# Context gate from two taps with three products per token pair, and the mixture gate's sums on VectorE

## What is computed

```python
ctx = causal_ema(x, tau_ctx)                       # h[t] = alpha * h[t-1] + x[t]
wg = sigmoid(concat([x, ctx], -1) @ Wg.T + bg)     # "wgate"
gated = x * wg
h1 = gelu(x @ Wn1.T + bn1)                         # "mod_hidden"
mod = 0.5 + sigmoid(h1 @ Wn2.T + bn2)              # "mod", one row per average
traces = [causal_ema(gated * mod[d], tau_raws[d]) for d in range(8)]
temporal = sum(traces[d] * softmax(blend, 0)[d] for d in range(8))
gate = sigmoid(temporal @ Wtemp.T + btemp)         # "tgate"
soma = gelu(x @ Wsoma.T + bsoma)
out = (soma * gate) @ Wout.T                       # "out"
x = x + layernorm(out) * gamma + beta

s0, s1, s2 = (relu(x @ share_wi[i]) @ share_wo[i] for i in range(3))
expert_out = two experts of the image's type, weighted by wa and wb
gi = concat([expert_out[:, 0], s0[:, 0], s1[:, 0], s2[:, 0]], -1)
g = softmax(relu(gi @ gate_w1) @ gate_w2, -1)      # the mixture's gate: one row of four per image
x = x + expert_out * g[0] + s0 * g[1] + s1 * g[2] + s2 * g[3]
```

## Time and profile before

| | |
|---|---|
| median of 3 runs | 1036.35 us (1035.94 to 1036.43) |
| the profiled execution | 1037.89 us, its span 1035.9 us |
| TensorE busy | 1029.4 us, 99% of the span, 4784 matmuls |
| VectorE busy | 806.9 us, 78% |
| ScalarE busy | 415.5 us, 40% |
| GpSimd busy | 16.4 us, 2% |
| moved to and from memory | 223 MB, 215 GB/s over the span |

### The profile page before, as it was taken

One profiled execution on the slowest core, in us unless ns is written; L12 is line 12 of the kernel. 1 busy time (PEld: TensorE's weight loads), 2 busy tenths in 40 slices (PEclk: granted clock), 3 DMA queues, 4 the chain that ended last, 5 costly groups with the idle time before them and its releaser, 6 DMA issues.

```text
span 1035.9 us, 12766 instructions
## 1 busy us (share of the span) xinstructions
PE 1029.4 (99%) x4784; PEld 853.9 (82%) x4784; DVE 806.9 (78%) x1369; ACT 415.5 (40%) x695; POOL 16.4 (2%) x26
## 2 busy tenths in 40 slices
PE   9999999999999999999999999999999999999998
PEld 6688888888888888888888888888888888888898
DVE  6989977799767988489785997659976699745236
ACT  7654455533344234422434233442333423333232
POOL 1200000000000000000000000000000000000000
PEclk9999999999999999999999999999999999999999
DMA  6388999786454754465544664546645475456581
GB/s 214 123 294 287 299 366 373 291 303 236 152 203 153 264 193 163 162 235 204 208 166 159 242 234 146 196 164 245 215 149 203 163 258 201 142 191 216 200 323 74
DMA packets 38304, 223.02 MB, mean 215 GB/s; under 512 B 4515, under 2 KB 5283, under 8 KB 16611
## 3 DMA queue, kind: packets, MB, share of 16 engines
q1 hardware_dynamic: 35938, 209.63, 56.9%
q0 software_dynamic: 2304, 12.58, 3.2%
HBM read 188.51 MB, written 33.69 MB: 215 GB/s over the span
## 4 chain that ended last, share of the span: by engine, by line
PE 95%; DMA 2%; DVE 2%; issue 0%; ACT 0%; SPq 0%; DVEq 0%
PE ps_up L680 14%; PE ps_up L710 14%; PE ps_up L711 14%; PE ps_down L752 14%; PE ps_down L753 14%; PE ps_down L756 14%; PE ps_aux L673 2%; PE ps_aux L674 2%; PE ps_aux L675 2%; DMA wi<-split_wi 1%; DVE y L1691 1%; DMA wo<-split_wo 1%; PE ps_aux L853 1%; PE ps_aux L850 1%; PE ps_aux L849 1%; PE ps_aux L833 1%
## 5 line engine op out<-in xcount | busy, mean ns | idle before, releaser
L1081 ACT ACTIVATE hid_hi<-ps_up 128x512 fp32r<-128x512 f32 (+1 forms) x336 | 193.6, 576 | 494.2 <-PE ps_up L680 493.4
L1344 DVE SCALAR_TENSOR_TENSOR hid_lo<-ps_up,hid_hi 128x512 fp32r<-128x512 f32 (+1 forms) x336 | 219.8, 659 | 170.6 <-ACT hid_hi L1081 169.9
L710 PE MATMUL ps_up<-x_hi_all,wi 128*128 128x512 f32 (+1 forms) x660 | 250.3, 381 | 0.3 <-DMA wi<-split_wi 0.3
L711 PE MATMUL ps_up<-x_hi_all,wi 128*128 128x512 f32 (+1 forms) x660 | 249.9, 380 | 0.0
L752 PE MATMUL ps_down<-hid_hi,wo 128*128 128x512 f32 (+1 forms) x640 | 245.4, 384 | 0.2
L753 PE MATMUL ps_down<-hid_hi,wo 128*128 128x512 f32 (+1 forms) x640 | 245.1, 384 | 0.0
L680 PE MATMUL ps_up<-x_lo_all,wi 128*128 128x512 f32 (+1 forms) x660 | 197.3, 380 | 0.2 <-DVE x_lo_all L1335 0.2
L756 PE MATMUL ps_down<-hid_lo,wo 128*128 128x512 f32 (+1 forms) x640 | 193.7, 384 | 0.0
L710 PEld LDWEIGHTS ps_up<-x_hi_all,wi 128*128 128x128 f32 x660 | 124.1, 188 | 24.6 <-DMA wi<-split_wi 1.0
L711 PEld LDWEIGHTS ps_up<-x_hi_all,wi 128*128 128x128 f32 x660 | 124.1, 188 | 23.1
L680 PEld LDWEIGHTS ps_up<-x_lo_all,wi 128*128 128x128 f32 x660 | 122.0, 188 | 24.2 <-DVE x_lo_all L1335 0.4
(11 more groups left out here) (259 smaller groups left out, 898.0 us busy)
## 6 DMA issues: line engine op xcount, KB each, us to landing
wi<-split_wi SPq DMA_DIRECT2D x70, 1024.0 KB, 4.9
wo<-split_wo SPq DMA_DIRECT2D x70, 1024.0 KB, 4.9
modb<-mod_scratch SPq DMA_DIRECT2D x28, 512.0 KB, 5.9
split_wi<-wi SPq DMA_DIRECT2D x10, 1024.0 KB, 7.4
split_wo<-wo SPq DMA_DIRECT2D x10, 1024.0 KB, 8.0
xt<-in_x SPq DMA_DIRECT2D x8, 512.0 KB, 5.7
split_wi<-ex POOLq DMA_DIRECT2D x4, 1024.0 KB, 9.6
split_wo<-ex POOLq DMA_DIRECT2D x4, 1024.0 KB, 4.9
```

What stands on the lines that cost most here:

```text
L710: pe.matmul(ps, w_hi, x2_hi[:, parity, c, tokens], start=c == 0, stop=False)
L711: pe.matmul(ps, w_lo, x2_hi[:, parity, c, tokens], start=False, stop=False)
L1081: act.activation(hid_hi[:, k % NU, tokens], ps_up[k % NU][:, tokens], ACT.Relu).then_inc(hid_hi_ready, 1)
L1344: dve.scalar_tensor_tensor(hid_lo[:, k % NU, tokens], ps_up[k % NU][:, tokens], 0.0, f32(hid_hi[:, k % NU, tokens]), ALU.max, ALU.subtract ...
```

## The change

**The context gate.** For n = 2 to 7 the tokens are taken in pairs. `xg_hi` and `xg_lo` hold all even tokens first and then all odd ones; results are put back in order where they are read out (`evens_odds`, `apart`). With `A` the weights for the token itself and `G` those for the token before it, an odd token `o` behind an even one `e` needs `A o + G e`, an even one behind the odd `p` needs `A e + G p`. Both contain `(A + G) e`, which is made once per pair (`gate_mid`, 12 matmuls of 256 columns, slot 3.5); the rest is `A (o - e)` and `G (p - e)` (24 matmuls of 256 columns, in `wgate`). The differences (`next_steps`) are made by VectorE and split into high and low part like all inputs. ScalarE copies the sum of `gate_mid` out of PSUM, and VectorE adds it to each half before the scan. The sum of the weights is made once: three additions on GpSimd (`add_gate_weights`), a rounding copy on ScalarE and a remainder on VectorE (`mid_weights`).

**The gate of the mixture.** `gate_part_hi`, `gate_part_lo` and the matmuls of `gate_hidden` go. VectorE adds over the partitions with transposes of 32x32 blocks and sums along the free axis (`gate_units`, then `gate_logits`, seventeen instructions), each behind the one before by a semaphore where it needs its result. The weights `gw2` are laid out for this on the host.

```diff
 PLAN_TENSOR = {
-    0.5: ["mod_hidden"], 1.5: ["soma"], 2.5: ["mod", "gate_hidden"], 4.5: ["wgate"],
+    0.5: ["mod_hidden"], 1.5: ["soma"], 2.5: ["mod"], 3.5: ["gate_mid"], 4.5: ["wgate"],
 PLAN_SCALAR = {
-    1: ["mod_hidden_low", "gate_part_hi"], 1.5: ["mod_hidden"], 2: ["soma"], 3: ["mod_low"], 3.5: ["mod"], 4: ["gate_exp"], 5.5: ["wgate"],
+    1: ["mod_hidden_low"], 1.5: ["mod_hidden"], 2: ["soma"], 3: ["mod_low", "gate_exp"], 3.5: ["mod"], 4: ["gate_mid"], 5.5: ["wgate"],
-    36: ["next_x_hi"],
+    36: ["next_x_hi"], 37.5: ["next_steps_hi"],
 PLAN_VECTOR = {
-    0.5: ["gate_part"], 1: ["mod_hidden_sum"], 2: ["mod_hidden_lo", "gate_part_lo"], 3: ["mod_sum"], 3.5: ["gate_logits"],
-    4.5: ["gate_soft", "mix1"], 5: ["wgate_scan"], 5.5: ["mix2", "mix3"], 6: ["gated"], 6.5: ["mix0"],
+    0.5: ["gate_part"], 1: ["mod_hidden_sum"], 1.5: ["gate_units"], 2: ["mod_hidden_lo", "gate_logits"], 3: ["mod_sum"],
+    3.5: ["gate_soft"], 4.5: ["mix1"], 5: ["wgate_scan"], 5.5: ["mix2", "mix3"], 6: ["gated"], 6.5: ["mix0"],
-    36.5: ["next_x_lo"],
+    36.5: ["next_x_lo"], 37: ["next_steps"], 38: ["next_steps_lo"],
 FIRST_PLANS (scalar)
-               31: ["ln_sqrt"], 34.5: ["turn"], 35.5: ["x2_hi"], 37: ["next_x_hi", "table_gelu"]},
+               31: ["ln_sqrt"], 34.5: ["turn"], 35.5: ["x2_hi"], 37: ["next_x_hi", "table_gelu"], 38: ["mid_weights"], 39: ["next_steps_hi"]},
 FIRST_PLANS (vector)
-               37.5: ["next_x_lo"]},
+               37.5: ["next_x_lo"], 38.5: ["mid_weights", "next_steps"], 39.5: ["next_steps_lo"]},
 LAST_PLANS
-    "tensor": {41.5: ["gate_hidden"]}, ... 40: ["gate_part"], 42: ["gate_logits"],
+    "tensor": {}, ... 40: ["gate_part"], 40.5: ["gate_units"], 41.5: ["gate_logits"],
...
 TensorE
+                elif step == "gate_mid":
+                    if n == 2:
+                        pe.wait_ge(mid_weights, 5)
+                    pe.wait_ge(aux_free[1], p.aux[1]["gate_mid"])
+                    for m in range(CT):
+                        for c in range(CT):
+                            at = slice(c * E + m * P, c * E + (m + 1) * P)
+                            mm = product(ps_aux[1][:, half(m)], mid_hi[:, at], mid_lo[:, at], xg_hi[:, c, half(0)],
+                                         xg_lo[:, c, half(0)], m == 0 and c == 0, m == CT - 1 and c == CT - 1)
+                    mm.then_inc(aux_ready[1], 1)
+                elif step == "wgate" and n > 1:
+                    pe.wait_ge(steps_ready, (n - 1) * 3)
+                    for m in range(CT):
+                        pe.wait_ge(aux_free[m], p.aux[m]["wgate"])
+                        for s, w in enumerate((W_GATE, W_SUM)):
+                            for c in range(CT):
+                                at = slice(w + c * E + m * P, w + c * E + (m + 1) * P)
+                                mm = product(ps_aux[m][:, half(s)], wc_hi[:, at], wc_lo[:, at], steps_hi[:, c, half(s)],
+                                             steps_lo[:, c, half(s)], s == 0 and c == 0, s == 1 and c == CT - 1)
+                        mm.then_inc(aux_ready[m], 1)
...
 ScalarE
+                elif step == "next_steps_hi":
+                    act.wait_ge(steps_ready, (n - 1) * 3 + 1)
+                    hi(steps_hi, token_steps).then_inc(steps_ready, 1)
+                elif step == "mid_weights":
+                    act.wait_ge(mid_weights, 3)
+                    hi(mid_hi, mid_raw).then_inc(mid_weights, 1)
+                elif step == "gate_mid":
+                    act.wait_ge(steps_ready, (n - 1) * 3)
+                    act.wait_ge(aux_ready[1], p.aux[1]["gate_mid"] + 1)
+                    act.activation(gate_mid, ps_aux[1][:, :], ACT.Copy).then_inc(aux_free[1], 1)
...
 VectorE
+                elif step == "next_steps":
+                    dve.wait_ge(x_loaded[(n + 1) % 2], ((n + 1) // 2 + 1) * 16)
+                    dve.wait_ge(ema_sum, n * (2 * D))
+                    for c in range(CT):
+                        even, odd = (evens_odds(x_of(n + 1)[:, c, :])[:, s, :] for s in range(2))
+                        to_even, to_odd = (token_steps[:, c, half(s)] for s in range(2))
+                        dve.tensor_scalar(to_even[:, 0:1], even[:, 0:1], -1.0, None, ALU.mult)
+                        dve.tensor_tensor(to_even[:, 1:HALF], odd[:, 0:HALF - 1], even[:, 1:HALF], ALU.subtract)
+                        last = dve.tensor_tensor(to_odd, odd, even, ALU.subtract)
+                    last.then_inc(steps_ready, 1)
+                elif step == "next_steps_lo":
+                    dve.wait_ge(steps_ready, (n - 1) * 3 + 2)
+                    lo(steps_lo, token_steps, steps_hi).then_inc(steps_ready, 1)
+                elif step == "mid_weights":
+                    dve.wait_ge(mid_weights, 4)
+                    lo(mid_lo, mid_raw, mid_hi).then_inc(mid_weights, 1)
+                elif step == "wgate_scan" and n > 1:
+                    dve.wait_ge(aux_free[1], p.aux[1]["gate_mid"] + 1)
+                    for c in range(CT):
+                        dve.wait_ge(aux_ready[c], p.aux[c]["wgate"] + 1)
+                        dve.tensor_tensor(evens_odds(gates[:, c, :]), apart(ps_aux[c][:, :]),
+                                          gate_mid[:, half(c)].rearrange("p (s k) -> p s k", s=1).broadcast_to([P, 2, HALF]), ALU.add)\
+                            .then_inc(aux_free[c], 1)
+                        dve.wait_ge(aux_free[c], p.aux[c]["wgate"] + 1)
+                        dve.tensor_tensor_scan(gates[:, c, :], alpha[:, D:D + 1].broadcast_to([P, T]), gates[:, c, :], 0.0,
+                                               ALU.mult, ALU.add).then_inc(gate_scanned, 1)
...
 GpSimd
+            def add_gate_weights():
+                pool.wait_ge(wi_ready, UNITS - 1)
+                pool.wait_ge(wc_ready[1], 1)
+                for t, place in ((wc_lo, mid_raw), (wc_hi, mid_raw_part)):
+                    pool.tensor_tensor(place, f32(t[:, W_GATE:W_SUM]), f32(t[:, W_SUM:W_SOMA]), ALU.add).then_inc(mid_weights, 1)
+                pool.wait_ge(mid_weights, 2)
+                pool.tensor_tensor(mid_raw, mid_raw_part, mid_raw, ALU.add).then_inc(mid_weights, 1)
...
             for j in range(0, TILES, 2):
                 keep_tile(j)
                 keep_tile(j + 1)
                 if j + 2 < TILES:
                     load_tile(j + 2)
                     load_tile(j + 3)
+                if j == 2:
+                    add_gate_weights()
```

More of the change, by code:

```diff
@@ L109 @@
 LAST_PLANS = {
[L110 to L111 removed]
+    "sync": {47: ["store0"], 55.5: ["store1"]}, "tensor": {}, "scalar": {43: ["gate_exp"]},
+    "vector": {40: ["gate_part"], 40.5: ["gate_units"], 41.5: ["gate_logits"], 43.5: ["gate_soft", "final_scale"],
                44.5: ["final_early0"], 45: ["final_early1"], 45.5: ["final_early2"], 46: ["final_early3"],
@@ L133 @@
 EDGE1 = 16
-AUX_BANKS = {"mod_hidden": (0,), "mod": (1,), "gate_hidden": (0,)}
-GATING = {"gate_hidden", "gate_part_hi", "gate_part_lo", "gate_logits", "gate_exp", "gate_part", "gate_soft",
+GATE_CHAIN = 17
+AUX_BANKS = {"mod_hidden": (0,), "mod": (1,), "gate_mid": (1,)}
+GATING = {"gate_units", "gate_logits", "gate_exp", "gate_part", "gate_soft",
           "mix0", "mix1", "mix2", "mix3", "store", "store0", "store1", "final_scale", "final_expert_a", "final_expert_b",
@@ L304, in build @@
         wgate_ready = sem("wgate_ready")
+        steps_ready = sem("steps_ready")
+        gate_scanned = sem("gate_scanned")
+        mid_weights = sem("mid_weights")
         gated_ready = sem("gated_ready")
@@ L421, in build, with evens_odds, apart @@
         turned = temporal[:, :, :].rearrange("p c (t a j) -> p a c t j", t=TT, a=4)
+        token_steps, steps_hi, steps_lo = trace[:, :, :], ct_hi[:, :, :], ct_lo[:, :, :]
+        gate_mid = trace[:, 0, :]
+        mid_raw, mid_raw_part = (raw_wi[:, 0, i * CT * E:(i + 1) * CT * E] for i in range(2))
+        mid_hi, mid_lo = mid_parts[:, 0, :], mid_parts[:, 1, :]
+        def evens_odds(tokens):
+            return tokens.rearrange("p (k s) -> p s k", s=2)
+        def apart(columns):
+            return columns.rearrange("p (s k) -> p s k", s=2)
         def x_of(n):
@@ L865, in beside @@
                         mm.then_inc(aux_ready[c], 1)
-                elif step == "gate_hidden":
-                    if later(p.aux[0]["gate_hidden"]):
-                        pe.wait_ge(aux_free[0], p.aux[0]["gate_hidden"])
-                    if final(f):
-                        pe.wait_ge(gate_part, f * 8 + 8)
-                        pe.matmul(ps_aux[0][:, 0:E], ones[:, :], gpart[:, :], start=True, stop=True).then_inc(aux_ready[0], 1)
-                    else:
-                        pe.wait_ge(gate_part_hi_ready, f + 1)
-                        pe.matmul(ps_aux[0][:, 0:E], ones_r[:, :], gpart_hi, start=True, stop=False)
-                        pe.wait_ge(gate_part_split, f + 1)
-                        pe.matmul(ps_aux[0][:, 0:E], ones_r[:, :], gpart_lo, start=False, stop=True)\
```

(33 more changed lines are left out.)

57 lines of the change are left out of this document (31 added, 26 removed).

## The result

The changed kernel takes 1040.46 us (median of 6 runs, 1039.8 to 1041.0), against 1035.89 us for the kernel before on the same chip: ratio 1.0037, 95% interval 1.0024 to 1.005. It is 4.6 us slower. The forecast was +4.4 us and 1040.8 us. A second series on another occasion gave 1040.13 against 1035.66 us (1.0048, 1.0035 to 1.0062). The profiled execution took 1040.37 us, with a span of 1038.4 us. That span is only 2.5 us longer than that of before (1035.9), because the profiled execution of before was itself 2.0 us over the median of its kernel. From there to the end the changed kernel is 4.2 us longer.

The account below looks back on a forecast made before the run. TensorE's matmul stream was taken to bound the kernel. Span: 1035.9 - 6.9 - 1.7 + 10.8 + 2.2 + 0 = 1040.3 us, +4.4; on the median 1036.35 that gives 1040.8 us, range 1036.5 to 1045.

Parts of the forecast that it names:

- The gate product: Context gate's matmuls on TensorE in images n = 2 to 7: 1.15 us less per image, 6.9 us in all.
- `gate_hidden`: Two matmuls of 256 columns removed from TensorE, 0.24 us, seven times: 1.7 us less.
- The last image: Float32 `gate_hidden` gives back 0.55 us, the longer gate chain may delay TensorE: between -0.55 and +0.5, taken as 0.
- The wait at the passage: From image 0 to image 1, TensorE's `down(1, 0)` waits for VectorE's expert sum behind GpSimd's late additions: +10.8 us, once.
- The clock: TensorE's clock falls after the idle stretch between image 0 and image 1, slowing matmuls: 0 to 4.4 us, taken as +2.2.
- The moving averages: VectorE's two extra additions per middle image lag 0.27 us, covered by 0.74 us of slack before a late `hid_lo`: 0.
- The additions are not late: Rival, 12%: GpSimd's three sums are done before ScalarE asks, leaving 2.7 us of chain at the passage: 1030.5 us.
- The clock stays high: Rival, 14%: TensorE's clock does not fall after the idle stretch, so the 2.2 us drop out: 1038.6 us.
- Every second element costs more: Rival, 13%: strided operands slow VectorE, up to 3 us in middle images and 1 in the chain: 1042 to 1045 us.

Follow-up runs that it names:

- mixture_gate_alone: The kernel before with only the mixture gate's part of the change, its context gate as before: 1034.12 us, ratio 0.998.
- adds_early: The changed kernel with GpSimd's three weight additions moved ahead of its stores of tiles 2 and 3: 1031.17 us; repeated, 1031.41 us.
- store_later: adds_and_steps_early with SyncE's store of image 0's output moved from slot 8 to slot 16 of the second image: 1026.53 us, ratio 0.9912.
- engine_kept_busy: The changed kernel with 46 unused float32 matmuls on TensorE during its wait for the expert sum before down(1,0): 1037.61 us, ratio 1.0014.
- adds_and_steps_early: adds_early with the first image's token differences moved to slots 32.5 to 34.5 and the weights' rounding to 36.5: 1028.79 us; repeated, 1028.23 us.
- one_addition_more: The changed kernel with a fourth, unused addition of 128x512 on GpSimd between the second and third: 1041.28 us, ratio 1.005.

## Why the prediction was right, and where it was off

- *The gate product, -6.9 us.* Right: 1.13 us an image against a forecast of 1.15, six images, 6.8 us.
- *`gate_hidden`, -1.7 us.* Right: 0.25 us an image, and 1.9 us for this part alone. The seventeen instructions took 3.7 us beside image 4 of the changed kernel, for an estimate of 3.4, and made nobody wait in the middle images.
- *The last image, 0.* The middle of the stated range, and about right. In the traces of the changed kernel and of mixture_gate_alone TensorE has one wait there that it didn't have before, for a `hid_lo` that VectorE comes to later, behind the gate's last steps and the mixing that follows them. Two matmuls start 0.50 us apart there instead of 0.12 (1025.74 and 1026.24), so 0.4 us of the 0.55 saved are lost again. In the changed kernel:

```profile
1026.24 0.50 PE L780 MATMUL ps_down<-hid_lo,wc_hi 128*128 128x256 f32 x2 [0.22 <-DVE hid_lo L1386]
```

  The 1.9 us of mixture_gate_alone contain it.
- *The wait at the passage, +10.8 us.* Right, at 10.9 us, and by the links named: the load's start, three additions, rounding, ReLU, `hid_lo`, the steps, ScalarE, VectorE, expert sum. The additions' lateness and the chain behind them were forecast at 8.1 and 2.7 us; adds_early leaves 2.2 us of wait, so they are 8.7 and 2.2. ScalarE's own wait was 9.9 us instead of the "about 7": I counted from the time its ReLU used to start, but ScalarE stood still from 169.5 us on. That changes no term, since the chain counts from the additions' end. The additions started at 175.54, not at 176.6, and TensorE arrived about as much sooner, as the opening was shorter in this execution.
- *The clock, +2.2 us.* Right in kind: the granted clock fell. That the size is near, 1.9 us, is partly luck, since 2.2 was only the middle between 0 and 4.4. The reading behind it, of slow matmuls in the opening as a low clock, stays an inference: the granted clock is 1.00 there, and no run tests it. The granted clock did fall at the passage.
- *The moving averages, 0.* Right, and the margin too. I had 0.74 us of slack, less 0.27. In the changed kernel the same `hid_lo` starts at 634.48 and takes 0.68 us, and its matmul starts at 635.83 with 0.23 us of weight load: 0.44 us left. An operand with every second element costs VectorE nothing, by the groups of the changed kernel:

```profile
L1528 DVE TENSOR_TENSOR gates<-ps_aux,trace 128x512 f32<-128x512 f32 x12 | 8.2, 680 | 1.7 <-PE ps_aux L699 1.7
...
L1377 DVE TENSOR_TENSOR xg_lo_all<-xt,xg_hi_all 128x512 fp32r<-128x512 f32 x12 | 7.7, 683 | 0.0
```

  That is the 684 ns of a plain pass over PSUM. The rule of the Trainium skill ("SBUF — State Buffer", section "Door 1: The DMA port swizzle") agrees with these rows of VectorE. ScalarE's rows agree less well: 720 ns against 688, as told at the end.
- *Not in the sum: a transfer, +0.6 us.* At 235.59 us of the changed kernel TensorE waits 0.95 us for `wi`, where it waited 0.29 us before (at 224.95). SyncE's and GpSimd's transfers keep the DMA engines full there (share 1.00 over the last 10 us ahead of the wait, in both kernels), and TensorE arrives 0.66 us sooner against the transfers: counted from the issue of the output's store on SyncE (209.83 before, 220.47 after), 14.17 us instead of 14.83. The wait is longer by as much, and store_later takes it away. This step was missed: I looked at what the change adds to queues, and not at who is waiting at the end of the stretch that it shortens.
- *The sum.* -6.8 - 1.9 + 10.9 + 1.9 + 0.6 is +4.7 us; measured are +4.6 and +4.5. That the forecast of +4.4 lies so near owes something to errors that cancel: the clock was put 0.3 too high, and the 0.6 of the transfer was left out.
- *The rivals.* "The additions are not late" was made true by adds_early: 1031.2 us, where I had 1030.5. Its own error is the clock. I took it to stay high behind a wait of 2.7 us, and it fell, for 1.6 us. "The clock stays high" was made true by engine_kept_busy, whose 1.9 us answer to the 2.2 of the forecast. "Every second element costs more" is refuted by the rows above.

Open: adds_and_steps_early should have been 8.6 us below the kernel before, less 0.6 for the transfer. By the medians it is 7.2 to 7.4 below. The traces put the missing 0.7 us outside the images: from the first copy of the expert weights to the end the two executions traced take 966.2 us, and that of before 974.7, 8.5 us more. The opening ahead of this copy took between 59.3 and 61.2 us in the fourteen traces, whatever the kernel. Only one trace of the kernel before exists, so what it usually takes there isn't known. Two of the six executions in the first series also had a mean granted clock of 0.998 and took 1030.1 and 1032.3 us, against 1027.0 to 1029.1 for the others; where they lost it, no trace shows.

## What to carry to other kernels

Of a step that is moved into another engine's queue, ask two things: what stands ahead of it there, and what stands behind the instruction that will wait for it. Here one rounding, wanted five slots later, stood ahead of two ReLUs and waited 9.9 us. Moving either the additions or the rounding, and the steps behind it, gave the whole wait of TensorE back and turned a loss of 4.6 us into a gain of 7 to 8, and of 9 with the store moved too. Where TensorE's stream gets shorter, look for the next transfer that it will reach sooner.

## What the runs showed of the hardware

- TensorE's granted clock fell toward the lower level, 1.2 GHz (0.53 to 0.59 of full speed in the windows), after a wait of 2.2 us in both traces of adds_early, not only after one of 10.9 us; two of that kernel's ten executions show hardly a fall or none. Behind the wait the matmuls stood about 0.43 us apart for 3.4 us (adds_early) to 5.2 us (one_addition_more), a loss of 1.6 to 2.4 us. A short wait of TensorE thus cost nearly twice its length here. Matmuls without use in the waiting time kept the clock at 1.00 in both cases. The Trainium skill ("TensorE: Matmul & The Clock Gate", section "What's actually happening") has the low clock as the state of rest, which activity releases; the traces agree, and a rest of 2.2 us was mostly enough in this kernel.
- ScalarE, unlike VectorE, paid a little for every second element: its `soma` of 128x512 took 720 ns where it had taken 688.
- GpSimd's addition of 128x512 in float32 took 1.25 to 1.30 us, and 1.03 us where both operands were the same (one instruction). The third of the three took 2.18 us where the additions stood early (154.61 us of adds_early, and 2.17 or 2.18 in the other traces with this order); no run shows why, and it cost nothing.
